# Layer 3 of a graph network beside the final loop of batch norm, and most of the layer-norm scales of layers 1 and 2 made one layer earlier

## The chip, the cores and the metric

The kernel runs on one core of a Trainium2 chip. Five engines work side by side and meet through semaphores only: TensorE (PE in the profile, its weight loads PEld), VectorE (DVE), ScalarE (ACT), GpSimd (POOL) and SyncE (SP, which here only starts transfers). The metric is the device time of one execution in microseconds; lower is better. Batches of 128 graphs with 128 nodes and 64 features each stay in the on-chip memory from the first layer to the last.

## The reference

Four layers, each on the layer-normed and rectified `h` of the running `x` (128 graphs x 128 nodes x 64 features), and each added to `x`:

```python
h = jnp.maximum(_layernorm(x, axis=-1), 0.0)
x = x + layer(h, adj, ...)
```

Layer 0 sums relu terms over neighbours (by gathers on TensorE), layer 1 has three rounds of `relu(adj @ (h @ W + b))` and a last linear map. The two that the change folds together are layer 2, which ends in a batch norm over all graphs, and layer 3:

```python
# layer 2
y = (adj @ h + h) @ weight + bias
y = y / jnp.maximum(norm(y), 1e-12)
mean = jnp.sum(y * m, axis=(0, 1)) / cnt
var = jnp.sum((y - mean) ** 2 * m, axis=(0, 1)) / cnt
y = relu(((y - mean) / jnp.sqrt(var + BN_EPS) * gamma + beta) * m)
# layer 3
messages = jnp.einsum('bij,bjh->bih', adjacency, h)
dh = jnp.tanh(concatenate([h, messages]) @ W1 + b1) @ W2 + b2
```

## The kernel before

The program is a row of blocks, one for a layer or a phase. In each block every engine has its own queue of instructions, written out by hand; a block begins when all engines have ended the one before. Graphs are handled in groups of 4 (`GS`), two groups at a time as a pair, `u` = 0 and 1, with buffers of their own; there are 16 pairs (`NI`). Batch norm goes over 16 chunks of 8 graphs (`NXC`, `GX`), each 128 partitions x 512 values.

**The scales of layer norm.** A layer norm needs two numbers for each node of each graph, `rstd` and `nmr`, in tiles with 128 columns, one column a graph. `stats(b)` makes statistics of one graph on VectorE (L279). `layernorm_var` makes variances of them (five small VectorE instructions, L255 to L262), `layernorm_std` takes a square root on ScalarE (L248), `layernorm_rstd` makes reciprocal and product on VectorE (L268, L270). Before layers 1, 2 and 3 this is done for all 128 graphs when the layer in front has ended. Then ScalarE normalises graph by graph, with L1130 (`norm_h1`) in layer 1 and L1139 (`norm_graph`) in layers 2 and 3, eight graphs ahead.

**Layer 1.** A pair goes through seven stages on TensorE for both halves in turn. ScalarE copies the results of stages 0, 1, 3 and 5 back (L1197, L1199), VectorE those of 2, 4 and 6 (L1239, L1254), and at the pair's end it adds the update to `x` (L1265). TensorE's L1169 is stage 0, L1165 stage 1.

**Batch norm's final loop.** For each chunk `c`: VectorE scales (`scale`, L1498), GpSimd adds beta (`shift_chunk`, L1556), ScalarE multiplies with the node mask and rectifies graph by graph (L1534), VectorE (even chunks, L1513) or GpSimd (odd chunks, L1565) adds to `x`, and VectorE makes the statistics of the new `x` (L279). TensorE has no part in it.

**Layer 3.** A block of its own. For each group TensorE sums over neighbours and transposes (`neighbours`, L1590, L1594), VectorE copies the sums (`copy_sums`, L1655), TensorE makes the hidden values (`hidden`, L1600, L1601), ScalarE takes tanh (L1642), TensorE makes the product (`product`, L1609), VectorE adds it and `x` (`update`, L1660, L1665), and SyncE stores the group. ScalarE loads the table of tanh at the start of the block.

Of the kernel before, what the change touches and what calls it, by code (L numbers as in the profile page):

```python
# [12 lines left out]
def gnn_stack_kernel(nc, a, out):  # L13
# [15 lines left out]
    GS = 4  # L29
# [19 lines left out]
    with ctx:  # L49
# [193 lines left out]
        halves = (slice(0, B // 2), slice(B // 2, B))  # L243

# [553 lines left out]
        with nc.Block() as block:  # L798
# [80 lines left out]
            def _(act):  # L879
# [20 lines left out]
                def step(b, g, u, q, nxt, p, use):  # L900
# [36 lines left out]
            def _(dve):  # L937
# [79 lines left out]
                def step(b, g, u, q, nxt, p, use):  # L1017
# [25 lines left out]
                    def late():  # L1043
# [103 lines left out]
        with nc.Block() as block:  # L1147
# [73 lines left out]
            def _(dve):  # L1221
                dve.wait_ge(s_bn0, 1)
                layernorm_scales(dve, 3)
# [78 lines left out]
        with nc.Block() as block:  # L1302
# [33 lines left out]
            def _(act):  # L1336
                layernorm_std(act, 4)
                act.wait_ge(s_ln, 4)
                for u in range(2):
                    for q in range(GS):  # L1340
                        norm_graph(s_hn2[u], u, GS * u, q, q == GS - 1)
                with act.Fori(0, NI - 1) as i:
# [6 lines left out]
            def _(dve):  # L1349
                v = nc.vector  # L1350
                dve.wait_ge(s_bn1, NI)
                layernorm_scales(dve, 4)
# [63 lines left out]
        s_xn = [sem(f"x_updated_layer2_{k}") for k in range(2)]  # L1416
        s_bn2 = sem("layer3_stats_made")
        AHEAD = 3
# [15 lines left out]
        def per_feature(t):  # L1434
            return t.unsqueeze(1).broadcast_to([N, GX, F])

# [12 lines left out]
        with nc.Block() as block:  # L1449
# [16 lines left out]
            @block.vector  # L1466
            def _(dve):
                v = nc.vector
                steps = [0]

                def settled(ins):
                    steps[0] += 1
                    ins.then_inc(s_vb, 1)
                    dve.wait_ge(s_vb, steps[0])

                dve.wait_ge(s_nrm, 1)
                settled(v.tensor_scalar(ss[:, :], ss[:, :], 1e-12, None, ALU.max))
                settled(v.reciprocal(ss[:, :], ss[:, :]))
                normalise(dve, v, 0)
                dve.wait_ge(s_ms, 1)  # L1480
                dve.wait_ge(s_cutmask, 3)
                v.tensor_tensor(blk, bank[0][0:GX, :], block_mask, ALU.mult).then_inc(s_blk, 1)
                dve.wait_ge(s_tot, 1)
                settled(v.tensor_reduce(stat[:, 0, :], bank[1][:, :].rearrange("p (g f) -> p f g", f=F), AX.X, ALU.add))
                v.tensor_scalar(stat[:, 1, :], stat[:, 0, :], rcnt[:, :], None, ALU.mult).then_inc(s_mean, 1)
                dve.wait_ge(s_mean, 1)
                centre(dve, v, 0)
                dve.wait_ge(s_dms, NXC)
                v.tensor_tensor(blk, bank[2][0:GX, :], block_mask, ALU.mult).then_inc(s_blk, 1)
                dve.wait_ge(s_tot, 2)  # L1490
                settled(v.tensor_reduce(stat[:, 2, :], bank[3][:, :].rearrange("p (g f) -> p f g", f=F), AX.X, ALU.add))
                settled(v.tensor_scalar(stat[:, 3, :], stat[:, 2, :], rcnt[:, :], None, ALU.mult))
                dve.wait_ge(s_var, 1)
                settled(v.reciprocal(stat[:, 5, :], stat[:, 4, :]))
# [221 lines left out]
```

## Time and profile before

| | us |
|---|---|
| three runs, median (lowest to highest) | 1461.05 (1458.61 to 1461.1) |
| the profiled execution, its own time | 1463.7 |
| span of its records | 1462.0 |
| TensorE busy | 1316.5 (90%) |
| VectorE busy | 1154.9 (79%) |
| ScalarE busy | 1105.1 (76%) |
| GpSimd busy | 502.5 (34%) |

The profile is of one execution. Its span runs from the first record to the last; the device time has 1.7 us more around it. Busy time of an engine is the sum of its instructions' times; matmuls are pipelined, so a busy TensorE is not TensorE at its peak. Layer 0 takes the span up to about 1005 us, layer 1 to 1226, layer 2's loop to 1284, batch norm to 1375 (its final loop from 1328), and layer 3 the rest.

### The profile page before, as it was taken

Reading aid. Unit: us, or ns where it says so; the run is one execution under the profiler, and the core shown is the slowest. Engines: PE = TensorE matmul, PEld = TensorE weight load, DVE = VectorE, ACT = ScalarE, POOL = GpSimd, SP = SyncE. Lnnn points to the kernel's source line nnn. Section 1 sums busy time; section 2 is a strip of 40 time slices with the busy share of each in tenths; the row PEclk is TensorE's granted clock in tenths of the full one; section 3 lists DMA queues with packets and bytes.
Section 4 is the critical chain, followed back from the end, with each engine's and each line's share of the span. In section 5 each row is a group of like instructions: output and inputs, shape, how many; then the busy total and the mean of one; then the engine's idle time right before and its main releaser. Section 6 shows DMA issues by size and latency. Waiting matters only on the chain. (4 is left out here: it accounts for less than half of the span.)

```text
span 1462.0 us, 41154 instructions
## 1 busy us (share of the span) xinstructions
PE 1316.5 (90%) x11243; PEld 1076.8 (74%) x11244; DVE 1154.9 (79%) x2874; ACT 1105.1 (76%) x2426; POOL 502.5 (34%) x611
## 2 busy tenths in 40 slices
PE   3999999999999999999999999997999997972398
PEld 1777777877777777777777777875889887910298
DVE  7898988899888988889888998883444445978755
ACT  4788888888888888888888888863555555916676
POOL 1343344444443344444433444431222111066400
PEclk9999999999999999999999999997999998986599
DMA  7000000000000000000000000000000000000022
GB/s 154 22 10 9 8 7 14 7 7 7 7 14 7 7 7 14 7 7 7 7 14 7 7 7 7 0 2 1 0 0 0 0 0 0 0 1 0 4 54 57
DMA packets 40925, 18.11 MB, mean 12 GB/s; under 512 B 19572, under 2 KB 40886, under 8 KB 40886
## 3 DMA queue, kind: packets, MB, share of 16 engines
q1 hardware_dynamic: 40354, 17.42, 4.8%
q8 instruction: 19, 0.31, 0.1%
q10 hardware_dynamic: 532, 0.21, 0.1%
q14 instruction: 20, 0.16, 0.0%
HBM read 13.44 MB, written 4.19 MB: 12 GB/s over the span
## 5 line engine op out<-in xcount | busy, mean ns | idle before, releaser
L723 DVE SCALAR_TENSOR_TENSOR acc<-slot_banks,acc 128x768 f32<-128x768 f32 x512 | 487.7, 953 | 79.5 <-PE slot_banks L442 70.6
L792 POOL TENSOR_TENSOR acc<-acc 128x384 f32<-128x384 f32 x128 | 128.1, 1001 | 529.1 <-DVE onediff L717 420.3
L442 PE MATMUL slot_banks<-ac_hi,work 128*128 128x192 f16 x1408 | 265.3, 247 | 27.3 <-DVE work L705 26.1
L442 PE MATMUL slot_banks<-ac_lo,work 128*128 128x192 f16 x1408 | 264.1, 246 | 0.0
L442 PEld LDWEIGHTS slot_banks<-ac_hi,work 128*128 (+1 forms) x1408 | 137.4, 98 | 98.4 <-issue 76.1
L442 PE MATMUL slot_banks<-ac_hi,onediff 128*128 128x192 f16 x1024 | 183.1, 246 | 6.4 <-DVE acc L723 5.1
L442 PE MATMUL slot_banks<-ac_lo,onediff 128*128 128x192 f16 x1024 | 182.3, 246 | 0.0
L442 PEld LDWEIGHTS slot_banks<-ac_lo,work 128*128 (+1 forms) x1408 | 138.2, 98 | 20.2 <-issue 14.5
L778 POOL TENSOR_TENSOR ac_lo<-ac,ac_hi 128x384 f16<-128x384 f32 x128 | 123.1, 961 | 49.3 <-ACT ac_hi L582 49.3
L542 ACT ACTIVATE work<-bank 128x512 f16<-128x512 f32 x256 | 130.7, 601 | 1.2 <-PE bank L353 1.2
L705 DVE TENSOR_SCALAR work<-work,slot_key 128x1024 f16 x256 | 117.9, 480 | 12.2 <-issue 3.7
L581 ACT ACTIVATE ac<-bank 128x384 f32<-128x384 f32 x128 | 62.2, 486 | 79.8 <-PE bank L402 79.8
L590 ACT ACTIVATE acc<-ac,neg_pad 128x768 f32<-128x768 f32 x128 | 119.3, 932 | 0.0
L442 PEld LDWEIGHTS slot_banks<-ac_hi,onediff 128*128 x1024 | 104.7, 102 | 16.7 <-issue 14.5
L606 ACT ACTIVATE slot_banks<-ac 128x768 f32<-128x768 f32 x127 | 103.5, 815 | 11.6
L402 PE MATMUL bank<-wac,hT 65*128 65x384 f32 x256 | 109.5, 510 | 1.7 <-ACT ac_hi L582 1.1
L599 ACT ACTIVATE work<-slot_banks 128x576 f32<-128x576 f32 x128 | 83.4, 651 | 34.9 <-PE slot_banks L442 33.3
L1218 POOL TENSOR_TENSOR adjT_all<-adjT_all,ident 128x512 f32 x32 | 39.9, 1269 | 176.1 <-PE slot_banks L1172 176.1
L442 PEld LDWEIGHTS slot_banks<-ac_lo,onediff 128*128 x1024 | 100.2, 98 | 0.0
L1139 ACT ACTIVATE onediff<-x_all,nmr,rstd 128x64 f32 (+1 forms) x256 | 90.7, 429 | 7.2 <-PE slot_banks L1310 2.9
L717 DVE TENSOR_TENSOR onediff<-work x128 | 88.6, 692 | 7.4 <-DVE work L705 0.6
L435 PE MATMUL slot_banks<-ac_hi,ident 128*128 128x384 f16 x258 | 85.1, 330 | 0.9 <-issue 0.7
(261 smaller groups left out, 3291.4 us busy)
## 6 DMA issues: line engine op xcount, KB each, us to landing
adj_in<-in_adj_dram SPq DMA_DIRECT2D x32, 256.0 KB, 2.8
out_dram<-acc SPq DMA_DIRECT2D x32, 128.0 KB, 2.0
l1w<-in_L_gnn_W_dram SPq DMA_DIRECT2D x2, 64.0 KB
l1b<-in_L_gnn_b_dram SPq DMA_DIRECT2D x2, 64.0 KB
x_all<-in_x_dram SPq DMA_DIRECT2D x4, 0.2 KB, 11.8
nm_in<-in_nodemask_dram ACTq DMA_DIRECT2D x1, 64.0 KB
w1a<-in_L_gnn_W_dram ACTq DMA_DIRECT2D x1, 48.0 KB
w1b<-in_L_gnn_W_dram ACTq DMA_DIRECT2D x1, 48.0 KB
```

Source lines behind the costliest of these rows:

```text
L402: nc.tensor.matmul(pAC[:, 0:2 * H], hT0[:, p, q * N:(q + 1) * N], wac[:, :], start=True, stop=True)\
L435: nc.tensor.matmul(unit(pair, t, n), node, part[:, q, 0:H].unsqueeze(1).broadcast_to([N, n, H]), start=(e == 0), stop=False)
L442: last = nc.tensor.matmul(unit(pair, t, 1), hot(t), part[:, q, H:2 * H].unsqueeze(1), start=False, stop=(e == 1 and (t % SB == SB - 1 or t ...
L542: last = nc.scalar.activation(rs[:, p, :, t, :], pA3[:, :].rearrange("p (q j) -> p q j", q=GS), ACT.Copy, bias=-float(t))
L590: nc.scalar.activation(acc[:, q, :].rearrange("p (t h) -> p t h", t=SU), ac32[:, q, 0:H].unsqueeze(1).broadcast_to([N, SU, H]), ACT.Relu, ...
L606: nc.scalar.activation(unit((q + 1) % 2, 0, SU), ac32[:, q, 0:H].unsqueeze(1).broadcast_to([N, SU, H]), ACT.Copy).then_inc(s_seed, 1)
L705: nc.vector.tensor_scalar(onehot[:, ds(at, CH)], ranks.rearrange("p t j -> p (t j)"), slot_key[:, ds(key, 1)], None, ALU.is_equal).then_in ...
L717: nc.vector.tensor_tensor(onediff[:, ds(at, CH)], onehot[:, ds(at, CH)], onehot[:, ds(at_old, CH)], ALU.subtract).then_inc(s_D, 1)
L723: nc.vector.scalar_tensor_tensor(out=sums, in0=unit((q + k) % 2, 0, SU), scalar=0.0, in1=sums, op0=ALU.min, op1=ALU.add).then_inc(s_free[k ...
L778: nc.gpsimd.tensor_tensor(ac_lo[:, q, :], ac32[:, q, :], ac_hi[:, q, :], ALU.subtract)\
L792: nc.gpsimd.tensor_tensor(acc[:, q, 0:2 * H], acc[:, q, 0:2 * H], acc[:, q, 2 * H:4 * H], ALU.add)
L1139: ins = nc.scalar.activation(hn[:, u, SLOT[q] * F:(SLOT[q] + 1) * F], x[:, ds((b + q) * F, F)], ACT.Relu, bias=nmr[:, ds(b + q, 1)], scale ...
```

## The change

Three edits.

1. **Layers 1 and 2: most of the scales one layer earlier.** The scales of graphs 0 to 95 (`most`) for layer 1 are made inside layer 0, in the steps of graphs 124 and 125; those for layer 2 inside layer 1, ahead of its last pair. In the next block ScalarE begins to normalise at once, and the scales of graphs 96 to 127 (`last_ones`) are made there beside it.
2. **Layer 3 in batch norm's block.** The block of layer 3 is gone. Its instructions stand among those of the final loop: pair `i` of layer 3 beside chunk `i + 5`. VectorE now scales, shifts (before GpSimd) and adds all chunks.
3. **The scales of layer 3 for 32 graphs at a time.** `variances` and `scales` on VectorE, with the inverse root by a power on GpSimd (`inverse_roots`) and a correction step on VectorE, in place of a square root on ScalarE.

The diff, cut to its core:

```diff
+        most, last_ones = slice(0, 3 * B // 4), slice(3 * B // 4, B)
...
@@ layer 0, ScalarE and VectorE
+                    if known(b) and b == B - GS + 1:
+                        layernorm_std(act, 3, most)
...
+                        if known(b) and b == B - GS:
+                            layernorm_var(dve, 3, most)
+                        if known(b) and b == B - GS + 1:
+                            layernorm_rstd(dve, 3, most)
...
@@ layer 1, ScalarE
-                layernorm_std(act, 3)
                 act.wait_ge(s_ln, 3)
                 for u in range(2):
                     for q in range(GS):
                         norm_h1(u, GS * u, q)
+                layernorm_std(act, 4, last_ones)
+                act.wait_ge(s_ln, 4)
...
                 with act.Fori(0, NI - 1) as i:
                     group_pair(i, True)
+                layernorm_std(act, 5, most)
                 group_pair(NI - 1, False)
...
@@ layer 1, VectorE
-                with dve.Fori(1, NI) as i:
+                with dve.Fori(1, NI - 1) as i:
                     group_pair(i, i - 1)
+                dve.wait_ge(s_bn1, 3 * NI // 4)
+                layernorm_var(dve, 5, most)
+                layernorm_rstd(dve, 5, most)
+                group_pair(NI - 1, NI - 2)
...
@@ batch norm's block, VectorE
+            v.tensor_tensor(g3(yc(c)), g3(yc(c)), per_feature(stat[:, 5, :]), ALU.mult).then_inc(s_ya, 1)
+            dve.wait_ge(s_ya, c + 1)
+            v.tensor_tensor(g3(yc(c)), g3(yc(c)), per_feature(beta[:, :]), ALU.add).then_inc(s_yb, 1)
...
+            dve.wait_ge(s_yc, 2 * c + 2)
+            v.tensor_tensor(xc(c), xc(c), yc(c), ALU.add).then_inc(s_xn, 1)
+            dve.wait_ge(s_xn, c + 1)
+            for e in range(GX):
+                last = stats(c * GX + e)
+            last.then_inc(s_bn2, 1)
+            if c % QC == QC - 1:
+                variances(dve, c // QC)
...
+                pool.wait_ge(s_lnq, 6 * k + 3)
+                g.tensor_tensor(std[:, cols], var[:, cols], minus_half[:, :], ALU.pow).then_inc(s_root, 1)
...
+            for c in range(3):
+                scale_and_shift(dve, c)
+            for c in range(LEAD - 1):
+                add_to_x(dve, c)
+                if c + 3 <= LEAD:
+                    scale_and_shift(dve, c + 3)
+                if c == QC - 1:
+                    scales(dve, 0)
+            copy_sums(0, 0)
+            for i in range(NI):
+                copy_sums(i, 1)
+                if i > 0:
+                    update(i - 1, 1)
+                if i + LEAD - 1 < NXC:
+                    add_to_x(dve, i + LEAD - 1)
+                if i + 1 < NI:
+                    copy_sums(i + 1, 0)
+                update(i, 0)
+                if i + LEAD - 1 < NXC and (i + LEAD - 1) % QC == QC - 1:
+                    scales(dve, (i + LEAD - 1) // QC)
+                if i + LEAD + 1 < NXC:
+                    scale_and_shift(dve, i + LEAD + 1)
+            update(NI - 1, 1)
...
@@ batch norm's block, ScalarE
+            def norm_group(i, u):
+                if u == 0 and i % QC == 0:
+                    act.wait_ge(s_ln3, i // QC + 1)
...
+            for i in range(NI):
+                for u in range(2):
+                    if i + 1 < NI:
+                        act.wait_ge(s_agg3[u], i + 1)
+                        norm_group(i + 1, u)
+                    act.wait_ge(s_lin3[u], i + 1)
+                    nc.scalar.activation(hid[:, u, 0:2 * N], bank[4 * u + 1][:, 0:2 * N], ACT.Tanh,
+                                         bias=l3b1[:, 0:1]).then_inc(s_tanh[u], 1)
+                    if i + LEAD < NXC:
+                        masked_relu(i + LEAD, u)
```

`LEAD` is 6 and `QC` is 4, so four chunks or pairs share one set of scales. The functions of layer 3 for TensorE (`neighbours`, `hidden`, `product`) move as they are into batch norm's block, and SyncE's stores too.

How the instructions stand on VectorE in the last phase, before: two chunks of the final loop, where `x_all` is the running `x`, `work` the batch-normed `y`, and every second addition is GpSimd's.

```order
L1498 TENSOR_TENSOR work<-work,acc 128x512
L1513 TENSOR_TENSOR x_all<-x_all,work 128x512
L279 BN_STATS bn<-x_all 128x6 x8
L1498 TENSOR_TENSOR work<-work,acc 128x512
L279 BN_STATS bn<-x_all 128x6 x8
```

And on VectorE in the changed kernel, one chunk together with one pair of layer 3 (`adj_in` holds the copied sums, `acc` the update):

```order
L1536 COPY adj_in<-bank 128x512
L1541 TENSOR_TENSOR acc<-x_all,l3b 128x256
L1546 TENSOR_TENSOR acc<-bank,acc 128x256
L1481 TENSOR_TENSOR x_all<-x_all,work 128x512
L280 BN_STATS bn<-x_all 128x6 x8
L1536 COPY adj_in<-slot_banks 128x512
L1541 TENSOR_TENSOR acc<-x_all,l3b 128x256
L1546 TENSOR_TENSOR acc<-slot_banks,acc 128x256
L1473 TENSOR_TENSOR work<-work,acc 128x512
L1475 TENSOR_TENSOR work<-work,beta 128x512
```

The six instructions of a pair of layer 3 now stand between the additions and scalings of batch norm, and the shift (L1475) is VectorE's.

ScalarE in layer 1, from the end of the loop over pairs through the last pair, before:

```order
L1205 COMPARE_AND_BRANCH
L1197 ACTIVATE work<-slot_banks 65x512
L1197 ACTIVATE work<-bank 65x512
L1199 ACTIVATE acc<-slot_banks 128x512
L1199 ACTIVATE acc<-bank 128x512
```

And in the changed kernel:

```order
L1213 COMPARE_AND_BRANCH
L249 ACTIVATE std<-var,eps_col 128x96
L1205 ACTIVATE work<-slot_banks 65x512
L1205 ACTIVATE work<-bank 65x512
L1207 ACTIVATE acc<-slot_banks 128x512
L1207 ACTIVATE acc<-bank 128x512
```

The square root for 96 graphs now stands ahead of the first copy of the last pair.

VectorE in layer 0, between the steps of graphs 124 and 125 in the changed kernel:

```order
L724 SCALAR_TENSOR_TENSOR acc<-slot_banks,acc 128x768
L256 TENSOR_TENSOR msum<-bn 128x96
L257 TENSOR_TENSOR dif<-bn 128x96
L258 TENSOR_TENSOR var<-bn 128x96
L260 SCALAR_TENSOR_TENSOR dif<-dif 128x96
L263 TENSOR_TENSOR var<-var,dif 128x96
L704 REGISTER_ALU
L705 ISA
L706 TENSOR_SCALAR work<-work,slot_key 128x1024
```

The five instructions are new; before, the one-hot (L705 there, the last row here) followed the sum (L723 there, the first row) at once.

## Rows read from the trace of the kernel before

**Rows 1.** Stages: us; PE, PEld, DVE, ACT, POOL busy; PEclk, DMA share, GB/s.

```profile
1328.00:1372.00 44.00, 0.00 (x0) 0.00 (x0) 43.97 (x155) 31.31 (x128) 36.77 (x24) 0.50 0.00 1
...
1400.00:1457.00 57.00, 57.00 (x424) 54.50 (x422) 34.07 (x71) 41.70 (x113) 0.00 (x0) 1.00 0.24 53
```

**Rows 2.** Timeline, seam of graphs 124 and 125: start us, us, engine, line.

```profile
976.05 0.87 DVE L705 TENSOR_SCALAR work<-work,slot_key 128x1024 f16 x2
...
977.35 0.25 PE L442 MATMUL slot_banks<-ac_hi,work 128*128 128x192 f16 x1
```

**Rows 3.** Timeline, start of layer 1: [idle before <- releaser].

```profile
1005.74 0.39 DVE L255 TENSOR_TENSOR msum<-bn 128x128 f32<-128x128 f32 x1 [0.33 <-PEq L798]
...
1009.15 2.76 ACT L1130 ACTIVATE work<-x_all,nmr,rstd 128x64 f32<-128x64 f32 x8 [1.35 <-DVE nmr L270]
```

**Rows 4.** Timeline, start of the last pair of layer 1.

```profile
1210.62 0.59 ACT L1197 ACTIVATE work<-slot_banks 65x512 f32<-65x512 f32 x1 [0.75 <-PE slot_banks L1169]
...
1210.76 0.76 DVE L1265 TENSOR_TENSOR x_all<-x_all,acc 128x256 f32 x2
...
1211.30 1.10 PE L1165 MATMUL slot_banks<-work,l1w 65*128 65x512 f32 x2
```

**Rows 5.** Timeline, start of layer 2.

```profile
1225.99 0.39 DVE L255 TENSOR_TENSOR msum<-bn 128x128 f32<-128x128 f32 x1 [0.32 <-PEq L1147]
...
1227.65 0.40 ACT L248 ACTIVATE std<-var,eps_col 128x128 f32<-128x128 f32 x1 [6.15 <-DVE var L262]
...
1229.40 2.76 ACT L1139 ACTIVATE onediff<-x_all,nmr,rstd 128x64 f32<-128x64 f32 x8 [1.35 <-DVE nmr L270]
```

**Rows 6.** Timeline, VectorE in the prologue, scales of 64 graphs.

```profile
24.65 0.27 DVE L255 TENSOR_TENSOR msum<-bn 128x64 f32<-128x64 f32 x1
...
25.57 0.22 DVE L262 TENSOR_TENSOR var<-var,dif 128x64 f32<-128x64 f32 x1
```

**Rows 7.** Timeline, final loop of batch norm.

```profile
1327.54 4.63 DVE L1498 TENSOR_TENSOR work<-work,acc 128x512 f32<-128x512 f32 x4
...
1337.33 1.75 DVE L1513 TENSOR_TENSOR x_all<-x_all,work 128x512 f32<-128x512 f32 x1
...
1340.02 0.73 DVE L1498 TENSOR_TENSOR work<-work,acc 128x512 f32<-128x512 f32 x1
...
1340.23 3.93 ACT L1534 ACTIVATE work<-work,nm 128x64 f32<-128x64 f32 x16 [0.59 <-POOL work L1556]
...
1340.67 1.10 DVE L279 BATCH_NORM_STATS2 bn<-x_all 128x6 f32<-128x64 f32 x8
...
1340.82 1.26 POOL L1556 TENSOR_TENSOR work<-work,beta 128x512 f32<-128x512 f32 x1 [0.63 <-DVE work L1498]
```

**Rows 8.** Timeline, start of layer 3.

```profile
1374.87 1.28 ACT L1629 ACT_TABLE_LOAD   x1 [1.60 <-PEq L1449]
...
1377.75 2.07 PE L1590 MATMUL slot_banks<-adjT_all,onediff 128*128 128x128 f32 x8 [52.55 <-ACT onediff L1139]
```

**Rows 9.** Timeline, VectorE and ScalarE in the last pair of layer 3.

```profile
1453.03 0.47 ACT L1642 ACTIVATE acc<-bank,l3b 128x256 f32<-128x256 f32 x1 [0.63 <-PE bank L1601]
...
1454.59 0.69 DVE L1655 COPY adj_in<-bank 128x512 f32<-128x512 f32 x1 [0.69 <-PE bank L1594]
...
1455.19 0.41 DVE L1660 TENSOR_TENSOR acc<-x_all,l3b 128x256 f32<-128x256 f32 x1
...
1455.89 0.42 DVE L1665 TENSOR_TENSOR acc<-bank,acc 128x256 f32<-128x256 f32 x1 [0.29 <-PE bank L1609]
...
1456.23 0.41 DVE L1660 TENSOR_TENSOR acc<-x_all,l3b 128x256 f32<-128x256 f32 x1
```

**Rows 10.** TensorE in the sums over squares: timeline, then stages as rows 1.

```profile
1307.14 16.16 PE L1461 MATMUL slot_banks<-work,nm 128*8 128x512 f32 x32 [2.68 <-ACT work L1527]
...
1307.00:1315.00 8.00, 7.86 (x14) 0.89 (x14) 8.00 (x6) 4.49 (x8) 8.00 (x6) 0.79 0.00 0
...
1315.00:1324.00 9.00, 8.30 (x19) 0.87 (x18) 3.82 (x3) 5.05 (x9) 4.29 (x3) 1.00 0.00 0
```

More of the change, by code:

```diff
@@ new lines, in variances @@
+        def variances(dve, k):
+            v = nc.vector
+            cols = slice(k * QG, (k + 1) * QG)
+            m0, q0, m1, q1 = (bn6[:, cols, t] for t in (1, 2, 4, 5))
+            dve.wait_ge(s_bn2, QC * k + QC)
+            v.tensor_tensor(msum[:, cols], m0, m1, ALU.add)
+            v.tensor_tensor(var[:, cols], q0, q1, ALU.add)
+            v.tensor_tensor(dif[:, cols], m0, m1, ALU.subtract).then_inc(s_lnq, 1)
+            dve.wait_ge(s_lnq, 6 * k + 1)
+            v.tensor_scalar(var[:, cols], var[:, cols], 1.0 / F, EPS, ALU.mult, ALU.add)
+            v.scalar_tensor_tensor(out=dif[:, cols], in0=dif[:, cols], scalar=0.25, in1=dif[:, cols],
+                                   op0=ALU.mult, op1=ALU.mult).then_inc(s_lnq, 1)
+            dve.wait_ge(s_lnq, 6 * k + 2)
+            v.tensor_tensor(var[:, cols], var[:, cols], dif[:, cols], ALU.add).then_inc(s_lnq, 1)
@@ new lines, in fold_in_act, with masked_relu @@
+        def fold_in_act(act):
+            def masked_relu(c, half):
+                act.wait_ge(s_yb, c + 1)
+                for b in range(c * GX + half * GX // 2, c * GX + (half + 1) * GX // 2):
+                    yb = y[:, b * F:(b + 1) * F]
+                    last = act.activation(yb, yb, ACT.Relu, scale=nm[:, b:b + 1])
+                last.then_inc(s_yc, 1)
+            def norm_group(i, u):
+                if u == 0 and i % QC == 0:
+                    act.wait_ge(s_ln3, i // QC + 1)
+                for q in range(GS):
+                    norm_graph(s_hn3[u], u, GS * grp(u, i), q, q == GS - 1)
+            nc.scalar.activation(cnt_col[:, 0:1], eps_col[:, 0:1], ACT.Tanh)
+            for c in range(LEAD - 1):
+                masked_relu(c, 0)
+                masked_relu(c, 1)
+            norm_group(0, 0)
+            norm_group(0, 1)
+            masked_relu(LEAD - 1, 0)
+            masked_relu(LEAD - 1, 1)
+            for i in range(NI):
[8 more added lines that the diff above has]
+                        masked_relu(i + LEAD, u)
@@ L1579, in gnn_stack_kernel @@
-        s_out = [sem(f"stored{u}") for u in range(2)]
-        with nc.Block() as block:
-            @block.tensor
-            def _(pe):
                 def neighbours(i, u):
@@ L1668, in pair, with settled @@
-                def pair(i):
-                    for u in range(2):
-                        ahead, behind = following(i, u), preceding(i, u)
-                        if ahead is not None:
-                            copy_sums(*ahead)
-                        if behind is not None:
-                            update(*behind)
-                copy_sums(0, 0)
-                pairs(dve, pair)
-                update(NI - 1, 1)
+                steps = [0]
+                def settled(ins):
+                    steps[0] += 1
+                    ins.then_inc(s_vb, 1)
+                    dve.wait_ge(s_vb, steps[0])
@@ new lines, in _ @@
+                dve.wait_ge(s_var, 1)
+                settled(v.reciprocal(stat[:, 5, :], stat[:, 4, :]))
+                settled(v.tensor_tensor(stat[:, 5, :], stat[:, 5, :], gamma[:, :], ALU.mult))
+                fold_in(dve)
+            @block.scalar
+            def _(act):
+                act.activation(ss[:, :], ss[:, :], ACT.Sqrt).then_inc(s_nrm, 1)
+                for c in range(NXC):
+                    act.wait_ge(s_d[c % 2], c // 2 + 1)
+                    if c >= 2:
+                        act.wait_ge(s_dms, c - 1)
+                    act.activation(tmp[:, 2 + c % 2, :], yc(c), ACT.Square).then_inc(s_dq, 1)
+                act.wait_ge(s_vb, 5)
+                act.activation(stat[:, 4, :], stat[:, 3, :], ACT.Sqrt, bias=eps_col[:, 0:1]).then_inc(s_var, 1)
+                fold_in_act(act)
```

231 lines of the change are left out of this document (95 added, 136 removed).

## The prediction, made before the result was known

> **What bounds the kernel now.** I read three views in this order: the busy time by stage, the timeline at the three seams between layers, and the timeline inside the two last loops. The stage rows show where TensorE has nothing to do: in the final loop of batch norm, 44 us long, it is busy 0.00 us while VectorE is busy 43.97 of 44 us; in layer 3 behind it TensorE is busy 57.00 of 57 us and VectorE 34.07 of 57 [rows 1]. So these are two stages with two different bounds, one behind the other. In the final loop each chunk of 8 graphs takes VectorE and GpSimd in turn, and a VectorE addition takes 1.75 us beside GpSimd against 0.73 us alone [rows 7]. In layer 3 a pair of groups has 2 x 18 matmul instructions, so by the stage's row 57.00 / 424 x 36 = 4.84 us, all of it TensorE's. At the two earlier seams, VectorE makes the scales of all 128 graphs while ScalarE and TensorE wait: the first activation of the next layer starts 3.41 us into the stage (1009.15 - 1005.74) and again 3.41 us (1229.40 - 1225.99) [rows 3, 5].
>
> **Layer 0's tail: +0.4 us.** Five small VectorE instructions for 96 graphs now stand between L723 and the one-hot L705 of graph 125. Their price: with 128 columns the five and the handover take 1227.65 - 1225.99 = 1.66 us [rows 5], with 64 columns 25.57 + 0.22 + 0.03 - 24.65 = 1.17 us [rows 6]; so about 1.42 us with 96 and 0.93 us with 32. The one-hot starts at 976.05, its first half is there by 976.5, and TensorE reads it at 977.35 [rows 2]: 0.9 us of cover, so 0.4 to 0.5 us comes through. The reciprocal and its product, one graph later, are about 1.0 us with 96 columns (seen as the stretch from L248 to the activation, 1229.40 - 1227.65 = 1.75 us with 128, less 0.4 for the root) and have cover of the same kind, so I add nothing. Bounds: 0, if TensorE's queue runs ahead more than here, and 2.4 us, if neither has cover.
>
> **Seam of layers 0 and 1: -3.4 us.** ScalarE's first eight activations wait for nothing any more; they start with the stage. The scales of the last 32 graphs (0.93 us, a root, 0.5 us) are made beside these eight activations and are waited for before the loop, whose first wait on TensorE ends later than that. Bounds: 3.0 to 3.4 us.
>
> **Layer 1's last pair: +2.5 us, and +1 for the clock.** This is the part with a new wait. ScalarE takes its root for 96 graphs ahead of the last pair, and the variances for it stand on VectorE behind the two additions that start at 1210.76 and end at 1211.51. So ScalarE waits until 1211.5 + 1.42 = 1212.9, spends about 0.35 us on the root, and makes its copy L1197 at 1213.2 and not at 1210.62. Behind it is the copy of the other half, and TensorE's L1165, which before started 0.09 us after the copy's end (1210.62 + 0.59 = 1211.21, 1211.30) [rows 4]. TensorE has no other work in this chain (groups 30 and 31 are the last), so the 2.6 us less the 0.1 of cover go through. TensorE is then idle for 2.5 us. After an idle time of 2.68 us the trace shows a stretch with a mean granted clock of 0.79 over 8 us, that is (1 - 0.79) x 8 x 2 = 3.4 us at the lower level, 1.2 GHz, before 1.00, 2.4 GHz, [rows 10]. If that happens here, 3.4 us at the lower level do the work of 1.7, so +1.7 us; if not, 0. I take 1. Bounds of the whole: 2.3 to 4.3 us.
>
> **Seam of layers 1 and 2: -3.4 us**, by the same reading as the first (1229.40 - 1225.99) [rows 5].
>
> **Batch norm's loop and layer 3.** VectorE now does everything in the loop but the masked relu: scale, shift, addition, statistics. From start to start, alone, a 128x512 operation takes 1340.67 - 1340.02 = 0.65 us and is done after 0.73 [rows 7]; a wait for the own result costs the rest and 0.04, so 0.12. Scale and shift of a chunk: 0.65 + 0.12 + 0.65 = 1.42 us. Addition and eight statistics: 0.65 + 0.12 + 1.02 (the row with 1.10, less an overlap of 0.08) = 1.79 us. The scales for 32 graphs: 1.0 us for six instructions with 32 columns, 0.9 us for four in a chain.
> (1) Until layer 3 starts, VectorE does 7 x 1.42 + 4 x 1.79 + 1.0 + 0.9 = 19.0 us from 1327.54 [rows 7], so to 1346.5. ScalarE's masked relu, 3.93/16 = 0.245 us each and 1.96 a chunk [rows 7], is faster than VectorE's 3.2 us a chunk. Four activations later (eight take 2.76 us [rows 5], so 1.4) TensorE starts, at 1347.9, where it now starts at 1377.75 [rows 8]. The table load of 1.28 us [rows 8] lies at 1326.6, beside VectorE's first chunks.
> (2) TensorE comes back at the low clock (eight matmuls in 2.07 us [rows 8]; the stage's mean is 57.00 / 424 = 0.13 us each with the wide ones). VectorE waits for its first two results, two times 2.1 us behind 1347.9 and 0.4 for the two transposes, until 1352.5.
> (3) Then VectorE sets the pace. A pair costs it 2 x 0.60 for the copies (1455.19 - 1454.59), 4 x 0.34 for the updates (1456.23 - 1455.89), twice 0.12 for the own result [rows 9], 1.79 for addition and statistics and 1.42 for scale and shift: 6.0 us against TensorE's 4.84 and ScalarE's 2 x (1.4 + 0.4 + 0.98) = 5.6 (its tanh takes 0.47 with the overlap [rows 9]). Eleven pairs carry additions, nine of them scale and shift, three the scales: 11 x 4.6 - 0.7 + 9 x 1.42 + 3 x 1.9 + 1 (cold start) = 69.4 us, to 1421.9.
> (4) Four more pairs are TensorE's again: 4 x 4.84 = 19.4 us. The last copy L1655 stands at 1441.3 and not at 1454.59 [rows 9]. What is behind it does not change. So -13.3 us; bounds -9 (0.4 us more of waits in each pair) and -15.
>
> **GpSimd's share.** Shift and half of the additions leave GpSimd. The Trainium skill bears on this: GPSIMD Engine Reference, section 4.1 Engine selection, has VectorE do elementwise additions, GpSimd being some 2x slower with two inputs. The trace agrees in direction, 1.26 against 0.73 us; the sum uses the trace's durations. New on GpSimd is a power with 32 columns. No row shows a power. From below it costs more than nothing; the dearest elementwise rows in this stage are 1.26 us alone, with 16 times the columns [rows 7]. VectorE has 1.4 us of other work (scale and shift, or a copy and an update) between giving the variances and asking for the roots. I take a power of at most 1.4 us, so nothing on the path.
>
> **Sum.** 0.4 - 3.4 + 3.5 - 3.4 - 13.3 = -16.2 us. The profiled execution took 1463.7 us around a span of 1462.0, so it would take 1447.5; against the median of the three runs, 1461.05, this gives 1444.9. I say 1445.
>
> **Rivals.**
> *The power is slow* (3 to 5.5 us). ScalarE may not go on with every fourth pair, and VectorE's four chains wait behind their cover of 1.4 us: each further us costs 4 us. At 3 us: 4 x 1.6 = +6.4, so 1451; at 5 us 1459. For it: nothing in the trace prices it, and a function evaluated by program can be far from an addition. Against: only 32 columns. Chance 0.10.
> *Slower than before: the power above 5.5 us.* Place: L1528 on GpSimd, four times, with VectorE waiting in scales() and ScalarE behind it. It decides from 16.2/4 + 1.4 = 5.5 us on (by over 0.2% from 6.2 us); at 8 us it is 4 x 6.6 = +26, 1471. Same evidence, further away. Chance 0.06.
> *TensorE's clock in the mixed stretch.* With VectorE at 6.0 us a pair, TensorE has 4.84 us of work and pauses in every group, up to 1.7 us where the scales are awaited. Where it is low all along, a pair takes about 2 x 4.84 = 9.7 us and eleven pairs lose 11 x 3.7 = 40 us, 1485; where it is low for half of the work, a pair takes 7.3 us and 11 x 1.3 = 14 us go, 1459. Against: low clock fills TensorE, which is what brought full clock back each time; and in the sums over squares, TensorE with short pauses (8.30 us busy of 9) stayed at 1.00 [rows 10]. The Trainium skill speaks for it: TensorE: Matmul & The Clock Gate, section A second HAM failure mode: psum-queue depth-cycling, tells of a kernel whose frequent small pauses between groups of matmuls made the clock go to and fro. By that rule the result is the 1459 of the half-low case; the rows at 1.00 here do not agree with it so far. Chance 0.09, a third of it slower than before.
> *More waits than counted.* Two engines near 6 us hand four results to each other in every pair; 0.4 us more in 11 pairs gives +4.4, 1449. Chance 0.15.
> *Forecast as it stands.* 0.60, its own range 1440 to 1449, from the bounds above: 1445 - 1.7 (scale of the last stage) - 1 (no low clock in layer 1) - a shorter cold start in layer 1, and + 2 (layer 0) + 2.
>
> **Chances.** 0.2% is 2.9 us, about what a measurement of this kernel can tell from no change. Above 1464: the power above 5.5 and a third of the clock, 0.06 + 0.03 = 0.09. Between 1458 and 1464: the rest of both rivals at their ends, 0.05. Faster: 0.86. The range is 1439 to 1456: above it lie the powers over 4.2 us (0.04 + 0.06) and most of the clock rival (0.07), below it 0.03.
>
> **What would show it.** In the changed kernel's trace: TensorE's first layer 3 matmul near 1345 (1347.9 less the seams' gains); a period of the copies L1536 of 6.0 us, 8 us where scales are made, 4.84 at the end; a granted clock of 1.00 in that stretch; ScalarE idle some 2.3 us ahead of the last pair's L1205, released by VectorE; the power L1528 under 1.4 us. The prediction is wrong if TensorE idles in the mixed stretch on ScalarE and not on VectorE, if VectorE's 128x512 operations stay above 0.8 us, or if either seam keeps a wait.

## The result, and the profile after

The changed kernel takes 1465.67 us in the median of 18 runs (1464.17 to 1467.79), the kernel before, run beside it, 1463.13 us (1458.46 to 1466.3). The ratio is 1.0022, with a 95% interval of 1.0012 to 1.0032. The forecast was 1445.0 us in a range of 1439 to 1456, so it failed: the change makes the kernel slower by about 3 us and not faster by 16. The profiled execution has a span of 1465.5 us, against 1462.0 before.

First the stages. These are windows of the changed kernel: start and end in us, length, busy time of each engine, TensorE's granted clock, DMA's share and rate.

```profile
1325.00:1342.00 17.00, 0.00 (x0) 0.00 (x0) 16.48 (x57) 10.72 (x42) 0.38 (x1) 0.54 0.00 0
1342.00:1350.00 8.00, 0.18 (x1) 0.18 (x2) 3.18 (x15) 1.66 (x5) 5.40 (x1) 0.50 0.00 0
1359.00:1372.00 13.00, 12.38 (x83) 10.89 (x81) 11.46 (x39) 10.61 (x37) 2.12 (x1) 1.00 0.18 40
1372.00:1380.00 8.00, 2.12 (x11) 2.09 (x11) 4.38 (x13) 3.68 (x13) 3.32 (x1) 0.63 0.08 17
1383.00:1401.00 18.00, 16.62 (x112) 14.62 (x111) 17.09 (x56) 15.98 (x55) 0.93 (x1) 1.00 0.20 45
```

The second, fourth and fifth rows are the story. From 1383 to 1401 us it goes as forecast: VectorE is busy 17.09 of 18 us, TensorE 16.62, the clock is 1.00. The two bounds of [rows 1] lie side by side there. But in the 8 us from 1342 and again from 1372, VectorE is busy 3.18 and 4.38 us, TensorE 0.18 and 2.12, and the clock is 0.50 and 0.63. What they wait for stands in the waits (engine, line and what it waited for; us in total, times, longest):

```profile
POOL std L1528 <- DVE var L1503: 96.0, 4, 25.1
PE slot_banks L1642 <- ACT onediff L1146: 44.4, 4, 26.8
ACT onediff L1146 <- DVE nmr L1517: 31.7, 4, 10.7
DVE dif L1511 <- POOL std L1528: 16.9, 4, 4.7
```

and the second of the four in the timeline (start, duration, engine, line, operation, output <- input, shapes; in brackets the idle time before it and who ended it):

```profile
1369.61 0.19 DVE L1503 TENSOR_TENSOR var<-var,dif 128x32 f32<-128x32 f32 x1
1369.72 0.68 DVE L1536 COPY adj_in<-slot_banks 128x512 f32<-128x512 f32 x1
1369.88 5.43 POOL L1528 TENSOR_TENSOR std<-var,minus_half 128x32 f32<-128x32 f32 x1 [22.48 <-DVE var L1503]
...
1370.84 0.42 DVE L1546 TENSOR_TENSOR acc<-slot_banks,acc 128x256 f32<-128x256 f32 x1
...
1375.35 0.19 DVE L1511 SCALAR_TENSOR_TENSOR dif<-std 128x32 f32<-128x32 f32 x1 [4.08 <-POOL std L1528]
...
1376.03 0.19 DVE L1517 SCALAR_TENSOR_TENSOR nmr<-msum,rstd 128x32 f32<-128x32 f32 x1
...
1376.32 1.44 ACT L1146 ACTIVATE onediff<-x_all,nmr,rstd 128x64 f32<-128x64 f32 x4 [6.71 <-DVE nmr L1517]
...
1377.92 2.07 PE L1642 MATMUL slot_banks<-adjT_all,onediff 128*128 x8 [5.88 <-ACT onediff L1146]
```

Read it downwards as one chain. VectorE gives the variances at 1369.8, GpSimd's power takes 5.43 us for 32 columns, VectorE has a copy and an update to do (until 1371.27) and then stands for 4.08 us. Its next instructions for TensorE, among them the other copy L1536, are behind the one that waits. So ScalarE waits 6.71 us and TensorE 5.88 us, and TensorE's first eight matmuls behind the gap take 2.07 us. That is the low level, 1.2 GHz; in [rows 8] the same eight took the same time behind the long idle time ahead of layer 3. In the first of the four waits (4.65 us) nothing runs at all but GpSimd.

At the seams the change does what it says. In the changed kernel the first activations of layers 1 and 2 start with VectorE's variances and no longer behind them ([rows 3, 5]: 3.41 us later); the last pair of layer 1 has the new wait ([rows 4] shows the place before):

```profile
1004.42 2.76 ACT L1137 ACTIVATE work<-x_all,nmr,rstd 128x64 f32<-128x64 f32 x8 [2.33 <-PEq L799]
1004.44 0.22 DVE L256 TENSOR_TENSOR msum<-bn 128x32 f32<-128x32 f32 x1 [0.33 <-PEq L799]
...
1206.70 0.32 DVE L256 TENSOR_TENSOR msum<-bn 128x96 f32<-128x96 f32 x1
...
1208.12 0.37 ACT L249 ACTIVATE std<-var,eps_col 128x96 f32<-128x96 f32 x1 [2.98 <-DVE var L263]
1208.40 0.57 ACT L1205 ACTIVATE work<-slot_banks 65x512 f32<-65x512 f32 x1
...
1209.03 1.12 PE L1172 MATMUL slot_banks<-work,l1w 65*128 65x512 f32 x2 [2.29 <-ACT work L1205]
...
1225.29 2.76 ACT L1146 ACTIVATE onediff<-x_all,nmr,rstd 128x64 f32<-128x64 f32 x8 [4.47 <-PEq L1154]
1225.31 0.21 DVE L256 TENSOR_TENSOR msum<-bn 128x32 f32<-128x32 f32 x1 [0.32 <-PEq L1154]
```

### The profile page after: what moved, and what is told of

It reads as the page before. It is cut to its first block and busy times, and to the rows that moved or that the text cites. A ratio compares the mean times of both kernels' runs of the same rounds, so it can differ in the third digit from the quotient of the medians.

```text
span 1465.5 us, 40775 instructions
## 1 busy us (share of the span) xinstructions
PE 1329.5 (91%) x11243; PEld 1083.7 (74%) x11244; DVE 1162.2 (79%) x2945; ACT 1101.5 (75%) x2427; POOL 487.7 (33%) x592
## 5 line engine op out<-in xcount | busy, mean ns | idle before, releaser
L443 PEld LDWEIGHTS slot_banks<-ac_lo,work 128*128 (+1 forms) x1408 | 138.0, 98 | 20.2 <-issue 14.6
L1146 ACT ACTIVATE onediff<-x_all,nmr,rstd 128x64 f32<-128x64 f32 (+1 forms) x256 | 91.2, 429 | 39.3 <-DVE nmr L1517 31.7
```

The source lines that it names most:

```text
L443: last = nc.tensor.matmul(unit(pair, t, 1), hot(t), part[:, q, H:2 * H].unsqueeze(1), start=False, stop=(e == 1 and (t % SB == SB - 1 or t ...
L1146: ins = nc.scalar.activation(hn[:, u, SLOT[q] * F:(SLOT[q] + 1) * F], x[:, ds((b + q) * F, F)], ACT.Relu, bias=nmr[:, ds(b + q, 1)], scale ...
```

## The experiments

My theory: everything but the power's duration went about as worked out. The rivals: the folded stretch loses by more and other waits or by TensorE's clock; the parts in the earlier layers cost the gain. All ratios are against the kernel before, run beside each version on the same chip; the chips differ between groups of runs, and the changed kernel's 1.0022 is its ratio from the section above, not run again. So versions are compared by their ratios, and a difference of ratios is given in us as that share of 1464 us.

### The power taken out

```diff
-                g.tensor_tensor(std[:, cols], var[:, cols], minus_half[:, :], ALU.pow).then_inc(s_root, 1)
+                g.tensor_tensor(std[:, cols], minus_half[:, :], minus_half[:, :], ALU.mult).then_inc(s_root, 1)
```

> The changed kernel with the four powers on GpSimd replaced by a product of two constants of the same 128x32 size; so the scales of layer 3 aren't the reference's. Theory (the power is the mis-sized term): GpSimd's instruction falls from 5.5 to under 0.5 us, VectorE's four waits for it (4.65 + 3 x 4.08 = 16.9 us) go, and with them the restarts of TensorE at the low clock behind the later three, some 1 us each: 1446 us, 1443 to 1450. Rival (the mixed stretch loses by more waits between the engines or by the clock even without the power): VectorE's waits go but the time stays at 1453 or more, with TensorE's granted clock under 0.95 in the pairs. Rival (the seams or the added instructions in the earlier layers cost the gain): 1455 or more.

Measured: 1447.75 us, ratio 0.9889 (0.9866 to 0.9912). GpSimd's instruction takes 0.24 us, and VectorE's wait for it is gone. 0.9889 is 16.2 us under 1464 (12.8 to 19.6 by the interval); 16.2 is also what my sum had for the whole change with a hidden power. Between this kernel and the changed one lie 0.0133 x 1464 = 19.5 us, with some 3.7 us of uncertainty, of them 16.9 the four waits. Ahead of layer 3's groups 8, 16 and 24 a pause is left, the chain of scales itself. These windows of this kernel are around the one at 1368 us:

```profile
1352.00:1366.00 14.00, 13.13 (x90) 11.63 (x88) 13.16 (x44) 13.45 (x46) 0.24 (x1) 1.00 0.18 39
1366.00:1370.00 4.00, 1.99 (x11) 1.71 (x12) 3.76 (x11) 2.02 (x7) 0.00 (x0) 1.00 0.16 35
1370.00:1388.00 18.00, 17.34 (x118) 15.34 (x117) 17.17 (x52) 16.79 (x58) 0.00 (x0) 1.00 0.20 44
```

TensorE idles 2 of 4 us, 1.71 of them in one pause, and many shorter times in the pairs, and the clock stays at 1.00. So the rival of the clock in the mixed stretch fell. The Trainium skill (TensorE: Matmul & The Clock Gate, section A second HAM failure mode: psum-queue depth-cycling) tells of a kernel whose frequent small pauses made the clock go to and fro; in this stretch the trace does not agree: pauses up to 1.71 us left it at 1.00, and in the changed kernel only the pauses of 5.88 us took it down.

### Each part by itself

*seams_alone* is the kernel before with the two early sets of scales, *fold_alone_cheap* the kernel before with the new end of the program and no power:

```diff
 # seams_alone: the end of the program as before
-                layernorm_scales(dve, 5)
+                layernorm_scales(dve, 7)
...
 # fold_alone_cheap: layers 0 to 2 as before, the new end, and in it
+                g.tensor_tensor(std[:, cols], minus_half[:, :], minus_half[:, :], ALU.mult).then_inc(s_root, 1)
```

> The kernel before with only the scales for 96 graphs ahead of layers 1 and 2; batch norm's loop and layer 3 as before. From the two traces: +0.8 in layer 0's tail, -3.4, +4.0 in layer 1's last pair, -3.4: -2.0 us against the kernel before. My forecast had these parts at -2.9. Rival (the early scales are what made the changed kernel slower): slower than before.

> The kernel before with only the end of the program changed (batch norm's loop and layer 3 folded), and the power again replaced by a product of constants, so the scales of layer 3 aren't the reference's. It measures one term of my sum by itself, -13.3 us for the fold. Theory (the mechanism and its size were right): -13 to -15 us against the kernel before, ratio 0.990 to 0.991. Rival (the fold is worth less, and the seams made up for it in the run with both): -10 us or less.

Measured: 0.9976 (0.9963 to 0.9988), so -3.5 us; and 0.9913 (0.9892 to 0.9933), so -12.7 us, in the medians 1449.35 against 1464.19. The intervals are 1.8 us to either side for the first and 3.0 for the second; my terms for the two were -2.9 and -13.3. The two measured values add up to the -16.2 of the run with both. The fold is worth what it was said to be, a little under the -13 to -15 that I expected for this run, and the early scales are no loss.

### What a power costs

```diff
+                g.memset(half, -0.5).then_inc(s_minus, 1)
+                g.memset(base, 0.7).then_inc(s_minus, 1)
...
+                for rows, width in [(N, n) for n in (4, 8, 16, 32, 64, 128)] + [(32, 32), (32, 128)]:
+                    for op in (ALU.pow, ALU.mult):
+                        g.tensor_tensor(power[0:rows, 0:width], base[0:rows, 0:width], half[0:rows, 0:width], op)                         .then_inc(s_minus, 1)
...
```

> The changed kernel, and on GpSimd behind its last power, where nobody waits for it, 16 instructions on constants: power and product in turn with 4, 8, 16, 32, 64 and 128 columns on 128 partitions, and with 32 and 128 columns on 32 partitions. It prices the power. If the cost is per column, 128x32 takes 5.4 us again, 128x128 some 20 us and 128x4 under 1 us; if it is a fixed cost of starting a program, all of them take about 5 us. The products should be under 0.7 us. The power's base is 0.7 here, in the kernel it is the variances.

The program took 1508.86 us in its one run, since these instructions last longer than layer 3; only their rows count here. The groups by shape, each with one power and one product in it (busy us, then the mean of the two in ns):

```profile
L1746 POOL TENSOR_TENSOR work<-work 128x128 f32<-128x128 f32 x2 | 21.4, 10695 | 0.2
L1746 POOL TENSOR_TENSOR work<-work 32x128 f32<-32x128 f32 x2 | 21.2, 10608 | 0.2
L1746 POOL TENSOR_TENSOR work<-work 128x64 f32<-128x64 f32 x2 | 10.9, 5436 | 0.2
L1746 POOL TENSOR_TENSOR work<-work 128x32 f32<-128x32 f32 x2 | 5.7, 2842 | 0.2
L1746 POOL TENSOR_TENSOR work<-work 32x32 f32<-32x32 f32 x2 | 5.7, 2831 | 0.2
L1746 POOL TENSOR_TENSOR work<-work 128x16 f32<-128x16 f32 x2 | 3.1, 1560 | 0.2
L1746 POOL TENSOR_TENSOR work<-work 128x8 f32<-128x8 f32 x2 | 1.8, 922 | 0.2
L1746 POOL TENSOR_TENSOR work<-work 128x4 f32<-128x4 f32 x2 | 1.4, 724 | 0.2
```

From 16 to 32 columns it is 2.6 us more, from 32 to 64 5.2, from 64 to 128 10.5: 0.164 us for each column, and nearly the same sums on 32 partitions as on 128. With 4 columns a fixed part shows: 1.4 us with the product, where I expected under 1 us for the power. The base is another than in the kernel, 0.7 in the place of the variances, and 128x32 takes the same 5.4 us (5.7 less a product of 0.24).

### More and less of it

```diff
 # power_half
+                half = slice(k * QG, k * QG + QG // 2)
+                rest = slice(k * QG + QG // 2, (k + 1) * QG)
+                g.tensor_tensor(std[:, half], var[:, half], minus_half[:, 0:QG // 2], ALU.pow)
+                g.tensor_tensor(std[:, rest], minus_half[:, 0:QG // 2], minus_half[:, 0:QG // 2], ALU.mult).then_inc(s_root, 1)
...
 # power_twice
+                g.tensor_tensor(std[:, cols], var[:, cols], minus_half[:, :], ALU.pow).then_inc(s_minus, 1)
+                pool.wait_ge(s_minus, k + 2)
                 g.tensor_tensor(std[:, cols], var[:, cols], minus_half[:, :], ALU.pow).then_inc(s_root, 1)
```

> The changed kernel with the power over 16 of each 32 columns only, and a product of constants for the other 16; so half of layer 3's scales aren't the reference's. By the sizes measured (0.164 us a column) the power takes about 2.7 us and the product 0.25. Theory (each us of the power above what VectorE does meanwhile costs 4 us of the whole): VectorE's four waits fall by 2.5 us each, to some 6.9 us in all, so 10 us less than the changed kernel, 1455 to 1457. Rival (most of the loss comes with the dependence on a third engine, whatever its length): within 4 us of the changed kernel.

> The changed kernel with each power made twice, the second behind the first. Theory: 5.4 us more in each of the four waits, 21.7 us more than the changed kernel, 1487; the longer idle time of TensorE adds nothing further for the clock. Rival (a part of the power's time is hidden, so the slope is under 4): 1480 or less.

Measured: 1458.17 us, ratio 0.9961 (0.9943 to 0.9978), and 1490.36 us, ratio 1.0184 (1.0153 to 1.0216). Against the changed kernel that is 8.9 us less and 23.7 us more, where the theory had 10 and 21.7 and the rivals at most 4 and about 14. VectorE's four waits are the first row in the half, the second in the doubled kernel:

```profile
DVE dif L1511 <- POOL std L1531: 7.5, 4, 2.3
...
DVE dif L1511 <- POOL std L1530: 38.9, 4, 10.2
```

Waits of 0, 7.5, 16.9 and 38.9 us go with 0, 10.5, 19.5 and 43.2 us of time over the kernel without a power (the ratios' differences times 1464). A us of wait costs a little more than a us, over the whole series 43.2 / 38.9 = 1.11, with some 5.8 us of uncertainty on the 43.2. So the power's duration is the cause of nearly all of the loss, and no part of it is hidden beyond the cover of 1.4 us.

### The clock, apart from the wait

```diff
+        FILL = 6
...
+                    if u == 0 and i > 0 and i % QC == 0:
+                        for _ in range(FILL):
+                            nc.tensor.matmul(bank[3][:, :], ident[:, :], adjT[:, 0:4 * N], start=True, stop=True)
                     pe.wait_ge(s_hn3[u], i + 1)
...
-                pairs(pe, pair)
+                for i in range(NI):
+                    pair(i)
```

> The changed kernel with the power and its waits as they are, but TensorE multiplies constants into a bank that nothing reads (six matmuls of 128x512, about 5 us at the high clock) where it waits for layer 3's groups 8, 16 and 24. It separates the clock from the wait. Theory (the wait counts, and the low clock behind it adds little because VectorE sets the pace again right after): clock 1.00 behind the three stalls and 1 to 3 us less than the changed kernel, 1463 us. Rival (the clock is half of the loss): 1458 or less.

Measured: 1462.23 us, ratio 0.9992 (0.9978 to 1.0007). VectorE's waits are the same 16.9 us, and the clock is 1.00 through all three stalls. The ratio is 0.0030 under the changed kernel's, 4.4 us, with some 2.6 us of uncertainty on that. I expected 1 to 3 us; the difference of the run without a power leaves 19.5 - 16.9 = 2.6 us for everything that is not the wait. The traces are sharper than the medians. These are the ends of VectorE's second and fourth wait in the changed kernel, and then in this one:

```profile
1375.35 0.19 DVE L1511 SCALAR_TENSOR_TENSOR dif<-std 128x32 f32<-128x32 f32 x1 [4.08 <-POOL std L1528]
...
1434.66 0.19 DVE L1511 SCALAR_TENSOR_TENSOR dif<-std 128x32 f32<-128x32 f32 x1 [4.08 <-POOL std L1528]
...
1374.74 0.19 DVE L1512 SCALAR_TENSOR_TENSOR dif<-std 128x32 f32<-128x32 f32 x1 [4.08 <-POOL std L1529]
...
1433.29 0.19 DVE L1512 SCALAR_TENSOR_TENSOR dif<-std 128x32 f32<-128x32 f32 x1 [4.08 <-POOL std L1529]
```

From the second to the fourth it takes 59.31 us and here 58.55; from the fourth to the end of the span (1465.5 and 1461.6) 30.84 and 28.31. By these two traces the low clock costs 0.8 us behind two stalls together and 2.5 us behind the last one, 3.3 us in all. The run without a power, with the other run's own two waits added to it, gives for the same stretch 3.4 us by the changed kernel's trace, and 4.2 to 4.6 by those of *variances_earlier*, *power_half* and *power_twice*; the split over the stalls differs (2.9 and 1.4 us in *variances_earlier*). So the low clock costs 3 to 5 us, and the wait is the larger part by far. TensorE's loop over the pairs is written out in this run, since the constants stand at three of them; between the first and the second wait, where no constants stand, it takes 27.56 us, against 27.92 in the changed kernel and 27.67 in *variances_earlier*.

### The power kept, and hidden

```diff
-        LEAD = 6
+        LEAD = 7
...
-                if c == QC - 1:
+                if c == QC:
                     scales(dve, 0)
...
-                if i + LEAD - 1 < NXC and (i + LEAD - 1) % QC == QC - 1:
-                    scales(dve, (i + LEAD - 1) // QC)
+                if i + LEAD - 2 < NXC and i > 0 and (i + LEAD - 2) % QC == QC - 1:
+                    scales(dve, (i + LEAD - 2) // QC)
```

> The changed kernel with the power kept, but asked for later: layer 3 starts one chunk further behind batch norm's loop (7 and not 6 chunks ahead), and VectorE asks for the roots one whole pair after it gave the variances (6 us of other work against 5.5 us of the power); at the start one chunk's addition, statistics, scale and shift lie between them (4.6 us). Theory (only the wait behind the power costs): three of the four waits vanish, the first falls from 4.65 to about 0.9 us; one pair more is TensorE's at 4.84 us in place of VectorE's 2.8 us for it, so 2 us more than with a cheap instruction: 1449 us, 1445 to 1453. Rival (the power itself disturbs VectorE or ScalarE while it runs, by a shared port or otherwise): VectorE's instructions beside it get longer and the time stays above 1455.

Measured: 1450.10 us, ratio 0.9907 (0.9884 to 0.9931). The powers take the same 5.43 us and VectorE's instructions beside them the same 0.68 us; VectorE waits twice and 2.0 us in all, ScalarE 13.0 us in the place of 31.7. So the power disturbs nobody but who asks for it too early.

### Layer 1's last pair

```diff
-                with dve.Fori(1, NI - 1) as i:
+                with dve.Fori(1, NI - 2) as i:
                     group_pair(i, i - 1)
                 dve.wait_ge(s_bn1, 3 * NI // 4)
                 layernorm_var(dve, 5, most)
+                group_pair(NI - 2, NI - 3)
                 layernorm_rstd(dve, 5, most)
```

> As scales_later, and in layer 1 VectorE makes the variances for 96 graphs one pair earlier, so that ScalarE's root ahead of the last pair waits for nothing. Theory (layer 1's last pair costs 4.0 us by that wait and the low clock behind it): ScalarE's wait of 2.98 us ahead of the last pair's copies goes, 3.5 us less than scales_later: 1445.5 us. Rival (the end of layer 1 has that pause anyway): within 1 us of scales_later.

> The changed kernel with the power and its waits, but the variances for 96 graphs made one pair earlier in layer 1. The difference of late_and_early and scales_later was 6.0 us, and in their traces the last pair lasts 18.39 us by the late and 15.37 us by the early variances from its first copy on, beside a wait of 2.5 us ahead of it. Theory: the last pair's part was 4 to 5.5 us and not 3.5: 1460 to 1461.5 us, 4 to 5.5 us less than the changed kernel. Rival (the 6.0 us were noise between the two): 2.5 us less or nothing.

Measured: with the hidden power 1444.09 us, ratio 0.9864 (0.984 to 0.9889), 0.0043 or 6.3 us under *scales_later*, with up to 5 us of uncertainty on that; with the power as it was 1462.99 us, 0.9991 (0.9976 to 1.0007), 0.0031 or 4.5 us under the changed kernel, with some 2.7 us. The traces are sharper here too. ScalarE's first copy of the last pair comes 12.95 us behind that of the pair ahead, as in the pairs before it, and no longer 15.45, so the wait was worth 2.5 us. The pair itself is shorter as well. From that copy to the next layer it takes 15.37 us here, as before [rows 4, 5]; 16.91 us in the changed kernel and in *power_half*; 18.39 us in the six other runs that have the wait. So the whole term is 4.0 us in two traces and 5.5 us in six. First copy and next layer of *late_and_early*, then those of *cheap_op*:

```profile
1204.31 0.59 ACT L1205 ACTIVATE work<-slot_banks 65x512 f32<-65x512 f32 x1 [0.48 <-PE slot_banks L1176]
1219.68 0.22 DVE L256 TENSOR_TENSOR msum<-bn 128x32 f32<-128x32 f32 x1 [0.32 <-PEq L1154]
...
1208.31 0.57 ACT L1205 ACTIVATE work<-slot_banks 65x512 f32<-65x512 f32 x1
1226.70 0.21 DVE L256 TENSOR_TENSOR msum<-bn 128x32 f32<-128x32 f32 x1 [0.32 <-PEq L1154]
```

### The best version found

*late_and_early*, and TensorE multiplies constants at the end of layer 1 and ahead of the starts of layers 2 and 3:

```diff
+        def keep_warm(count):
+            for _ in range(count):
+                nc.tensor.matmul(bank[3][:, :].rearrange("p (q j) -> p q j", q=GS), ident[:, :],
+                                 ident[:, :].unsqueeze(1).broadcast_to([N, GS, N]), start=True, stop=True)
...
+                keep_warm(3)
...
+                keep_warm(1)
                 neighbours(0, 0)
...
+                pe.wait_ge(s_lnq, 3)
+                keep_warm(7)
                 neighbours(0, 0)
```

> late_and_early, with TensorE kept busy by matmuls of constants into a bank that nothing reads: seven (128x512) ahead of layer 3 from the first variances on, three at the end of layer 1, one at the start of layer 2. Theory (the restart at the low clock costs, where nothing else sets the pace): layer 3's first eight matmuls take 1.05 and not 2.08 us, layer 2's too: 1.5 us less at each of the two places, 1441 us. Rival (VectorE and ScalarE set the pace there anyway): within 1 us of late_and_early, 1444.

Measured: 1441.44 us, ratio 0.9855 (0.9835 to 0.9875). TensorE's rows at the start of layer 3:

```profile
1333.69 8.67 PE L1144 MATMUL slot_banks<-ident 128*128 128x512 f32 x14 [18.46 <-DVE var L1511]
1342.20 1.05 PE L1650 MATMUL slot_banks<-adjT_all,onediff 128*128 128x128 f32 x8
```

Layer 3's first eight matmuls take 1.05 us. The ratio is 0.0009 or 1.3 us under that of *late_and_early*, and the intervals overlap widely, so a gain by the constants is not shown. Against the kernel before this version is 1.45% faster, some 21 us.

## Why the prediction was wrong

The step that failed is **GpSimd's share**: "I take a power of at most 1.4 us, so nothing on the path." It is 5.43 us (5.78 the first time), and the four waits for it put 16.9 us and the low clock behind them on the path. I had taken the dearest elementwise row of the stage as the nearest one and counted on 32 columns being few. That row's 1.26 us for 512 columns is 0.0025 us a column; a power's column costs 0.164, 66 times as much. Few columns were no bound, since no row showed that the price of a column was of the same kind.

The **rivals** had the place and the mechanism, the chain from L1528 through `scales()` to ScalarE, with 0.10 and 0.06 of the chance. Their price was too low: 4 us for each us above the cover, deciding from 5.5 us. At 5.43 us that gives 4 x 4.0 = 16.1 us, near the 16.9 of the four waits, and a change that breaks even. What it lacks is the low clock behind them, 3 to 5 us, which I had counted for the rival of the mixed stretch and for layer 1 but not here. With 3 us for it the change breaks even, by my estimate, at a power of about 1.4 + (16.2 - 3) / 4 = 4.7 us, and 5.43 is on the other side. One of the signs that I named came up too: in the stalls TensorE waits for ScalarE (5.88 us), but ScalarE waits there for VectorE (6.71) and VectorE for GpSimd (4.08), so it is the same chain.

Point by point:
- **Layer 0's tail, +0.4.** The small one-hot operation L712 of graph 124, ahead of the insertions, starts at 974.01 us in the changed kernel and at 974.96 in the kernel before (its L711); that of graph 127, behind them, at 995.08 and 995.15. A lead of 0.95 us has shrunk to 0.07, so the two insertions cost about 0.9 us. Between the two, at graph 125, the lead is 0.55 (981.29 and 981.84): the variances cost the 0.4 us of the sum, and the rest is the reciprocal's, to which I gave nothing.
- **Both seams, -3.4 each.** Shown: the activations start with the stage, in both.
- **Layer 1's last pair, +2.5 and +1.** The wait is 2.98 us for ScalarE and 2.29 for TensorE, as worked out. The clock was mis-sized: 16.91 - 15.37 = 1.5 us in the profile of the changed kernel, 3.0 in six other traces, so 4.0 or 5.5 us for the whole term in place of 3.5. The 3.4 us at the lower level that I took from [rows 10] are those of the changed kernel (below: (0.30 + 0.27) x 3 x 2 = 3.4 us); in *cheap_op* they are 6.8. The runs without the wait (4.5 and 6.3 us) agree with that, but do not exclude 3.5 by themselves.
- **Batch norm's loop and layer 3, -13.3.** Measured by itself -12.7 us. The price of an undisturbed VectorE operation held: the additions, 1.75 us beside GpSimd before, take 0.68 us. (The 0.73 us that I set beside it from [rows 7] is a scaling of the same size, not an addition.) The first layer 3 matmul stands at 1349.82, and less the wait of 4.65 us that is 1345.2, where I had it near 1345. The copies L1536 on one bank follow at 1383.71, 1389.69 and 1395.67, a period of 5.98 us for the forecast 6.0. The clock is 1.00 in the pairs.
- **Sum.** Everything but the power gave -16.2 us by the run without it, the number of the prediction. That the two agree to the last digit is luck: with the terms as measured the sum is 0.9 - 3.4 + 4.0 - 3.4 - 12.7 = -14.6 us, or -13.1 with the 5.5 us of that run's own trace, and its interval is 3.4 us to either side. The early scales by themselves measured -3.5 us (-5.3 to -1.7), where their terms as measured give -1.9 or -0.4; what makes up the rest is not known.

What stays open: why the low clock behind the same pause lasts longer in some executions (below), what a difference of 1 to 3 us between two versions is worth beside that, and whether a power with fewer columns at a time would do still better than the later request; that was not tried.

## What to carry to other kernels

An operation of a kind that the trace does not show has no nearest row: bound it by what it must be to turn the result, and give that bound its chance, however small the tile is. If a slow instruction stands on an engine that has little else to do, leave it there, give its inputs early and ask for its result late; here one chunk more of lead and a request one pair later were worth 17 us (1.0022 against 0.9907). And count a wait that stops TensorE as those of 2.3 and 5.9 us did here twice, once for itself and once for the low clock behind it: 1.5 or 3.0 us behind the one, 3 to 5 us behind the three others together.

## What the runs showed of the hardware

GpSimd's power costs 0.164 us a column, on 32 partitions as on 128; a product of 128x32 takes 0.24 us. Behind the pause of 2.3 us in layer 1's last pair the low level held for different times: these are three windows of 3 us from 1209 us on in the changed kernel, and then the same of *cheap_op*, with the same instructions.

```profile
1209.00:1212.00 3.00, 2.97 (x7) 1.48 (x8) 0.54 (x2) 1.33 (x3) 0.00 (x0) 0.70 0.00 0
1212.00:1215.00 3.00, 3.00 (x22) 3.00 (x22) 1.21 (x2) 0.32 (x1) 0.00 (x0) 0.73 0.00 0
1215.00:1218.00 3.00, 3.00 (x28) 2.92 (x26) 1.37 (x6) 1.19 (x2) 0.00 (x0) 1.00 0.01 3
...
1209.00:1212.00 3.00, 3.00 (x6) 1.41 (x7) 0.45 (x2) 1.08 (x3) 0.00 (x0) 0.64 0.00 0
1212.00:1215.00 3.00, 3.00 (x16) 3.00 (x15) 0.69 (x1) 0.48 (x1) 0.00 (x0) 0.50 0.00 0
1215.00:1218.00 3.00, 3.00 (x21) 3.00 (x20) 1.20 (x5) 0.78 (x2) 0.00 (x0) 0.72 0.01 3
```

The clock is back at 1.00 by 1215 us in the one and after 1215 in the other, which is the difference of 1.5 us between the two last pairs. As their instructions up to there are the same, the difference is one of the execution and not of the kernel.

The start of layer 1, where TensorE has also been idle, shows it again. This is the stretch from 1014 to 1018 us in the kernel before, and then in *fold_alone_cheap*, which has the same instructions up to the end of layer 2 and began layer 1 2.15 us sooner (1003.59 and 1005.74):

```profile
1014.00:1018.00 4.00, 4.00 (x9) 1.85 (x8) 0.00 (x0) 1.20 (x3) 0.00 (x0) 0.50 0.00 0
...
1014.00:1018.00 4.00, 4.00 (x36) 3.98 (x35) 1.38 (x2) 2.06 (x5) 0.00 (x0) 1.00 0.00 0
```

Every pair of layer 1 without a new wait takes 12.95 us from one first copy to the next, but the first pair takes 16.2 to 16.5 us in some traces (16.51 in the kernel before, 16.46 in the changed one) and 13.3 to 14.4 in others (13.51 in *fold_alone_cheap*, 13.46 in *late_and_early*). A restart of TensorE is thus worth up to 3 us more or less by chance. With several of them in the kernel that would go a long way to the 8 us over which the times of the kernel before are spread, though that was not tested; and no single pair of traces can price a change of 1 to 3 us in this kernel by its whole span.
